# Merged last stage of a four-layer convolution chain: conv2 of a tile, its update and its squares come three turns behind the tile's scaling instead of five

## The reference

```python
def _gn(v, G=8, eps=1e-5):        # mean and variance of each image and group
    ...
# --- layer 0 ---  1x1 mix of channels, leaky relu, min-max scaling per plane
x = x + _L0_conv_ref(_gn(x), L0_conv_w, L0_conv_b)
# --- layer 1 ---  real FFT, complex 3x3 convolution of the spectrum, inverse FFT
x = x + _L1_conv_ref(_gn(x), ...)
# --- layer 2 ---  3x3 convolution, zero padding, on values rounded to 8-bit steps
x = x + _L2_conv_ref(_gn(x), L2_conv_weight_int8, L2_conv_scale_weight, L2_conv_bias)
# --- layer 3 ---  3x3 convolution with circular padding (written as FFTs)
x = x + _L3_conv_ref(_gn(x), L3_conv_weight)
```

## Time and profile before

| what | value |
|---|---|
| median of 3 runs | 6660.71 us (6643.02 to 6668.57) |
| the profiled execution, its own time | 6655.92 us |
| its span, first to last instruction | 6653.9 us |
| mean granted TensorE clock | 0.952 of full |
| PE busy | 5695.1 us, 86% of the span |
| DVE busy | 4982.8 us, 75% |
| ACT busy | 4486.0 us, 67% |
| merged last stage, about | from 4565 us to the end |

### The profile page before, as it was taken

The page is one execution under the profiler, slowest core; times in us unless marked ns, Lnnn a source line. Parts: engine busy times, 40 slices in busy tenths (PEclk is TensorE's granted clock), DMA queues, the critical chain, the costliest instruction groups (busy, mean ns, idle before and its releaser), DMA issues. The chain is left out here.

```text
span 6653.9 us, 202054 instructions
## 1 busy us (share of the span) xinstructions
PE 5695.1 (86%) x64138; PEld 3662.2 (55%) x64138; DVE 4982.8 (75%) x9849; ACT 4486.0 (67%) x8680; POOL 2750.1 (41%) x4633
## 2 busy tenths in 40 slices
PE   0259989989988988988998997994889889889889
PEld 0027757757756766765775774872334334334334
DVE  6867887887887887877887887788667667667664
ACT  0367766766767767767766556555878778778776
POOL 2136555556556646546556555650111111111112
PEclk9979999999999999999999998998999999999999
DMA  5325634633643652651661551553667667667665
GB/s 177 121 59 151 185 101 129 185 123 110 185 141 92 186 159 74 185 177 56 184 188 35 143 140 38 143 143 60 170 164 202 166 172 207 170 163 207 165 173 137
DMA packets 535618, 959.15 MB, mean 144 GB/s; under 512 B 121946, under 2 KB 126682, under 8 KB 532826
## 3 DMA queue, kind: packets, MB, share of 16 engines
q1 hardware_dynamic: 471898, 815.99, 44.0%
q10 hardware_dynamic: 63104, 134.23, 6.5%
HBM read 560.66 MB, written 287.60 MB: 127 GB/s over the span
## 5 line engine op out<-in xcount | busy, mean ns | idle before, releaser
L1575 PE MATMUL pC<-xs,taps 128*128 128x512 f16 x4608 | 1094.2, 382 | 108.1 <-DMA xhalo<-xs 100.4
L872 PE MATMUL pM<-gw,xh 64*128 64x256 f16 (+1 forms) x24960 | 1126.1, 244 | 0.0
L872 PEld LDWEIGHTS pM<-gw,xh 64*128 64x128 f16 x24960 | 964.6, 95 | 129.1 <-issue 2.9
L607 POOL TENSOR_TENSOR X<-X,zo 128x256 f32 (+1 forms) x512 | 371.9, 726 | 1243.5 <-DVE X L1019 1243.5
L1575 PEld LDWEIGHTS pC<-xs,taps 128*128 128x128 f16 x4608 | 448.4, 98 | 670.9 <-DVE xs L1624 88.3
L1471 POOL TENSOR_TENSOR xn<-xn,one_col 128x1 f32<-128x1 f32 x520 | 175.2, 337 | 1367.4 <-ACT xn L1505 1367.4
L778 PE MATMUL pM<-X,mix0s 64*64 64x512 f32 x2304 | 533.1, 638 | 179.8 <-DVE X L991 108.2
L592 POOL TENSOR_TENSOR X<-X,rl 128x512 f32 x384 | 478.2, 1274 | 397.0 <-ACT rl L638 396.7
L1491 ACT ACTIVATE scaled<-X,qbias,qscale 128x512 f32 (+1 forms) x512 | 410.9, 804 | 338.8 <-DMA X<-after_layer 277.8
L1513 ACT ACTIVATE xs<-xn 128x1028 f16<-128x1028 f32 x520 | 545.7, 1049 | 89.3 <-POOL xn L1472 88.7
L1019 DVE SCALAR_TENSOR_TENSOR X<-pZ,X 128x512 f32 (+1 forms) x512 | 353.8, 691 | 327.6 <-ACT zo L667 326.4
(11 more groups left out here) (236 smaller groups left out, 13781.1 us busy)
## 6 DMA issues: line engine op xcount, KB each, us to landing
gw<-row_weights SPq DMA_DIRECT2D x520, 288.0 KB, 3.4
after_layer<-X SPq DMA_DIRECT2D x512, 256.0 KB
out_dram<-result SPq DMA_DIRECT2D x512, 256.0 KB
stage<-in_x_dram SPq DMA_DIRECT2D x224, 512.0 KB
X<-in_x_dram SPq DMA_DIRECT2D x448, 256.0 KB
X<-after_layer ACTq DMA_DIRECT2D x224, 512.0 KB, 5.7
xhalo<-xs SPq DMA_DIRECT2D x504, 96.4 KB, 3.8
qhalo<-q SPq DMA_DIRECT2D x496, 96.2 KB, 4.0
```

What stands on the lines that cost most here:

```text
L607: nc.gpsimd.tensor_tensor(X[:, j, 0], X[:, j, 0], zo[:, k], ALU.add)
L872: nc.tensor.matmul(pY[:, r, col:col + nd * P], row(xh, r)[:, k, p, ri, off:off + P], weights(r, q_, d, nd, ri), start=ri == 0 and off == 1 ...
L1575: nc.tensor.matmul(bank, taps3[:, d, wh], xs[:, h, own, d:d + W], start=d == 0 and n == 0, stop=False)
```

## The change

Three steps of layer 2 move two turns forward on their engines: `conv2` of tile w goes from turn w + 17 to w + 15, `update` from turn w + 18 to w + 16, `square3` from w + 19 to w + 17. The scaling, clipping and rounding of a tile, its halos, the whole of layer 3, the loads and the stores stay in the turns in which they were. A round has 81 turns instead of 83. Ring slots and semaphore values are shifted to fit. No instruction is added or taken away.

```diff
-                TURNS = DELAY + J + 7 
+                TURNS = DELAY + J + 5 
...
-                            if c2 and live(u, 7, J + 7):
-                                square3(b + 1, u - 7, k)
+                            if c2 and live(u, 5, J + 5):
+                                square3(b + 1, u - 5, k)
...
                     def conv2(b, w, k, g):
-                        slot = (k - 1) % RING
+                        slot = (k + 1) % RING
...
-                        done = w // RING if isinstance(w, int) else g - 3 + (k + 7) // 8
+                        done = w // RING if isinstance(w, int) else g - 2 + (k + 1) // 8
...
-                            nc.tensor.matmul(pC2[:, slot % 4], taps2[:, d], q[:, k, d:d + W], start=d == 0, stop=False)
+                            nc.tensor.matmul(pC2[:, slot % 4], taps2[:, d], q[:, (k + 2) % RING, d:d + W], start=d == 0, stop=False)
...
-                            w, v = t - DELAY - 5, t - 6
+                            w, v = t - DELAY - 3, t - 6
...
-                        nc.vector.scalar_tensor_tensor(out=Xf[:, w], in0=pC2[:, (k - 2) % 4], scalar=oscale2[:, :], in1=Xf[:, w],
+                        nc.vector.scalar_tensor_tensor(out=Xf[:, w], in0=pC2[:, k % 4], scalar=oscale2[:, :], in1=Xf[:, w],
...
-                            if c2 and live(u, 6, J + 6):
-                                update(b + 1, u - 6, k)
+                            if c2 and live(u, 4, J + 4):
+                                update(b + 1, u - 4, k)
```

## The result

The changed kernel takes 7447.72 us in the median of 4 runs (7441.89 to 7455.33), against 6656.72 us for the kernel before in the same comparison: a ratio of 1.1183, with a 95% interval of 1.116 to 1.1206. The forecast was 7565 us with a range of 7200 to 7900 us. The profiled execution has a span of 7444.7 us, 790.8 us more than before, and a granted clock of 0.917.

The account below looks back on a forecast made before the run. The prediction took PE to bound the merged rounds and a closed halo ring to replace it: 6655.92 us + 800 (merged rounds) + 107 (layer 2 alone) = 7563, about 7565 us for the median, range 7200 to 7900 us.

Parts of the forecast that it names:

- What bounds the kernel: Merged rounds, kernel before: PE itself is the bound, working 6.91 of 7.02 us per pair of turns.
- The halo: Merged rounds: conv2 waits for L1409 each odd turn, closing a two-turn ring of 6.4 us plus landing, 9.7 us a pair.
- The landing: L1409 from issue to landing: taken as 3.3 us, between bounds of 2.7 and 4.2 us.
- The clock: PE after idle waits in merged rounds: some matmuls run at 1.2 GHz, adding 1.4 us, so 11.1 us a pair.
- Rival 2: Merged rounds: each critical turn runs at half clock, 13.1 us a pair, 7955 us in total; chance 8%.
- Layer 2 alone: First piece, without layer 3: same ring at slow clock, 6.3 us a pair instead of 2.94, +107 us.
- The drain and the shorter round: Round ends, where only layer 2 is left: losing two turns changes nothing, 0 within 3 us for a round.
- The sum: Whole kernel: 6655.92 us plus 800 for merged rounds plus 107 for layer 2 alone gives 7563 us.
- The signs named beforehand: Changed kernel's profile: merged windows near 310 us, conv2 halo waits of 2 to 4 us, load and store waits nearly gone.
- rival 1: Merged rounds: the ring closes but the clock stays at 2.4 GHz, 7146, 7263 or 7440 us by landing; chance 15%.
- Rival 3: Whole kernel: halo arrives in time and shorter rounds make it faster, 6600 to 6642 us; chance 2%.
- Rival 4: Merged rounds: the ring is looser than read, a pair between 7.02 and 9.1 us, 6700 to 7100 us; chance 3%.

Follow-up runs that it names:

- the best variant: Kernel before with clip and quant ahead of finish on DVE and layer 2's halo transfers ahead of the last turn's store: 6600.96 us, ratio 0.9915.
- experiment 5: Changed kernel plus nine unread matmuls ahead of the waiting conv2 of each odd merged turn: 7280.25 us, ratio to the kernel before 1.0938.
- experiment 1: Changed kernel with clip and quant ahead of finish on DVE: 6959.53 us, ratio to the kernel before 1.0454.
- experiment 4: Changed kernel with layer 2's two halo transfers issued in the other order: 7550.78 us; same edit on the kernel before, as control: 6675.69 us.
- distance four: Kernel before with conv2, update and square3 one turn earlier instead of two, order as before: 6706.05 us, ratio 1.0074.
- experiment 2: Changed kernel with clip and quant ahead of finish, and layer 2's halo transfers ahead of the previous turn's store on SP: 6827.19 us, ratio 1.026.

## Why the prediction was right, point by point

- **What bounds the kernel.** PE in the merged rounds, 6.91 of 7.02 us. It held: what made PE wait went into the time, and the best variant ends at 6.92 us.
- **The halo.** The step was that conv2 in odd turns waits for a transfer issued behind the last DVE instruction of the turn before, and that DVE is held by PE, so that a ring of two turns closes. Three runs with different edits show it: a longer way round through DVE's order takes away 488 us, one turn more through single halos 711 us, and 0.63 us more in the ring adds 0.63 us a pair in the piece with layer 2 alone, where the clock stays low throughout. The parts were read nearly rightly: "2.66 + 0.1 + 3.66 plus the landing" with the measured landing of 2.8 gives 9.2 us, against 9.5 us in the median from one waiting conv2 to the next in experiment 5, at a clock of 0.99. Its timeline says where the 0.3 us are: conv2 to finish takes 3.80 us instead of 3.66, finish to the issue of the transfer 2.67, as read, and the issue to the first matmul 3.02 instead of 2.9 (medians).
- **The landing, mis-sized.** "I take 3.3 us" was 0.5 us too much; it measured 2.8, close to the lower end of the bounds. It was argued from the share of the DMA engines, 0.48, and that share was 0.55. The share is no good guide: in experiment 1 it was 0.60 to 0.64 and the landing 4.4 us, in experiment 5 it was 0.59 to 0.60 and the landing 2.8 us. What differs more plainly is the place: in the changed kernel L1409 comes after a pause of SP, with nothing issued for several us, and in experiment 1 it is issued right behind a store and two other halos. But one transfer right ahead of it is not enough to delay it: in experiment 4 the transfer that conv2 waits for follows the other one after 0.6 us, and both land after 2.7 us in the median. What sets the landing stays open.
- **The clock, mis-sized.** "I take 1.4 us" for a pair measured 0.84 us by experiment 5. Both levels occur, as the earlier trace rows had shown (the 1.23 us read there as 1.2 GHz lie between 0.81 and 1.44 us, so only part of those three matmuls was slow): in the changed kernel nearly all waits in front of conv2, but for the first of each round and those in the drains, are 1.7 to 2.7 us long, and some are followed by slow matmuls and some are not. These PE rows of the first merged round show both after a wait of the same length, and the windows the clock from each conv2 to the next:

```profile
4827.98 1.46 PE L1562 MATMUL pC<-q,taps 128*128 128x512 f16 x3 [2.22 <-DMA qhalo<-q]
...
4838.90 0.81 PE L1562 MATMUL pC<-q,taps 128*128 128x512 f16 x3 [2.21 <-DMA qhalo<-q]
```

```profile
4827.98:4838.90 10.92, 8.71 (x33) 3.46 (x34) 5.27 (x13) 6.60 (x11) 0.66 (x4) 0.85 0.53 133
4838.90:4848.58 9.68, 7.08 (x32) 3.03 (x33) 5.67 (x14) 6.35 (x10) 0.66 (x4) 0.99 0.64 154
```

  A slow start costs 10.92 - 9.68 = 1.24 us here. Over the 196 pairs of the merged rounds, the pairs that began slow took 10.88 us in the median and 11.04 in the mean, the others 9.66 and 9.64: 1.2 to 1.4 us more, so no more than what the prediction took as the least. It had priced a slow start at 2.4 us, the middle between that least and a critical turn that is slow throughout. And 103 of 196 starts were slow, not two of three. They were not spread at random: among 189 pairs that follow one another, 159 times a slow start came next to one at full clock. With waits of nearly one length, what PE had done in the pair before went with the level; why is not shown.

  In the kernel that the Trainium skill describes, page "TensorE: Matmul & The Clock Gate", section "HAM oscillation — how this bites in real kernels", the waits are about 3 to 5 us long and every round starts slow. This trace agrees for waits of that length: all 14 conv2 of the merged stage that waited more than 3.3 us were slow. For the shorter waits of the ring it was about half. Rival 2 made of it that the whole critical turn is slow in each pair; it gave 7955 us and is 507 us off.
- **Layer 2 alone.** +107 us forecast, +103.9 us measured, and the clock stayed low there (0.61), as was taken. A pair took 197.83 / 32 = 6.2 us, where 6.3 was forecast.
- **The drain and the shorter round.** "0, within 3 us for a round": 0.7 us over all seven.
- **The sum.** 800 us for the merged rounds against 646.3 + 39.9 us. (7563 + 4.8 is 7568; the forecast says about 7565.) The two mis-sized terms, 0.5 us for the landing and 1.4 - 0.84 = 0.56 us for the clock, make 196 x 1.06 = 208 us too much by themselves. About 94 us came back, and no term of the forecast had foreseen them: the ring is 0.3 us a pair longer than its parts, some 55 us, and the first wait of each round was 7.0 us in the mean where the forecast counted 2.8 us, another 29 us. The last 10 us stay open. So it is partly luck that the forecast of 7565 us is only 117 us off.
- **The signs named beforehand.** The windows last 289 us where "near 310" was named, as the pair was too long in the forecast. Waits for loads fell from 277.8 to 49.0 us in front of L1491, and those for stores from 234.9 to 38.4 us in front of L1631. That DVE's finish waits for PE in nearly every turn, and not in every second one, was not foreseen.
- **Rivals.** That the clock stays full (rival 1) is excluded by the windows, whose clock is 0.90, though the measured time of 7448 us is the 7440 us which that rival gave with landings of 4.2 us: two errors that cancel, which the time alone could not have told from the forecast. Rival 3 needed a landing of 0.7 us; the fastest took 2.7. Rival 4 would have left the time under 7100 us.

## What to carry to other kernels

Before a consumer is moved closer to its producer, follow what it waits for back to the instruction that the producer's engine itself waits for: if this closes a ring, count its turns and divide its length by them. Here the ring at distance four cost 0.7%, and the one of two turns 11.8%. A transfer that is sent for two tiles at a time leaves the ring only as many turns as its worse tile has, and it allows only an even number of turns. The order within a turn counts too, on the computing engine and on the queue that issues the transfer: in the changed kernel a better order took back 488 and then 132 us, and in the kernel before it was the gain. If an idle time can't be avoided on TensorE, its length is not its whole price.

## What the runs showed of the hardware that had not been expected

- Matmuls that nobody needs made the program 167 us faster (experiment 5), by holding the granted clock at 0.99 instead of 0.90 through waits that were otherwise mostly 1.7 to 2.7 us long.
- After waits of 2.21 and 2.22 us the same three matmuls took 0.81 and 1.46 us. The length of the wait alone does not decide the clock. Slow and full-clock starts mostly alternated from one pair to the next.
- The same transfer of 96 KB landed after 2.8 us in the median when SP had paused ahead of it, and after 4.4 and 4.5 us in experiments 1 and 2, in which it was issued right behind others. The share of the DMA engines was 0.60 both with a landing of 2.8 us (experiment 5) and with one of 4.4 us (experiment 1).
